# Holding the early loads of a retrieval kernel behind landings of its gathers

## The reference

```python
retrieved = jnp.mean(item_embeddings[indices], axis=1)       # 512 x 512, from 50 rows each
fused_input = jnp.concatenate([user_rep, retrieved], axis=1) # 512 x 1024
fused_rep = fused_input @ W_fuse + b_fuse                    # W_fuse 1024 x 512
logits = fused_rep @ W_proj + b_proj                         # W_proj 512 x 12500
```

## Time and profile before

| | |
|---|---|
| runs | 305.96, 305.21, 304.99 us |
| median | 305.21 us |
| the profiled execution's own time | 304.82 us |
| its span (first to last instruction) | 303.0 us |
| TensorE matmul busy | 290.6 us (96%) |
| VectorE busy | 242.4 us (80%) |
| ScalarE busy | 159.8 us (53%) |
| GpSimd busy | 73.1 us (24%) |
| DMA bytes moved | 75.14 MB |
| granted TensorE clock | 1.00 |

### The profile page before, as it was taken

How to read it: one execution, slowest core, us unless ns; L and a number is a source line. 1 busy time by engine, 2 the same in 40 slices (tenths; PEclk the granted TensorE clock), 3 DMA queues, 4 the chain that set the end, 5 groups by cost and what they waited for, 6 DMA issues and landing times.

```text
span 303.0 us, 4031 instructions
## 1 busy us (share of the span) xinstructions
PE 290.6 (96%) x1351; PEld 236.1 (78%) x1351; DVE 242.4 (80%) x355; ACT 159.8 (53%) x217; POOL 73.1 (24%) x76
## 2 busy tenths in 40 slices
PE   3996999999999999999999999999999999999995
PEld 1446887888888888888778888888888888888884
DVE  5897999668667789769998979979799797995133
ACT  3005665544544558968465685556845568453310
POOL 4785786777777100000000000000000000000000
PEclk9999999999999999999999999999999999999999
DMA  7999999896997247558875939749397493443315
GB/s 259 359 390 297 406 382 379 301 369 240 313 384 267 78 136 212 184 163 323 280 280 180 352 130 296 284 153 351 136 291 284 153 364 129 144 154 115 130 70 203
DMA packets 32480, 75.14 MB, mean 248 GB/s; under 512 B 4445, under 2 KB 20587, under 8 KB 32460
## 3 DMA queue, kind: packets, MB, share of 16 engines
q1 hardware_dynamic: 25340, 58.31, 54.6%
q0 software_dynamic: 5536, 13.73, 13.2%
q10 hardware_dynamic: 1584, 2.84, 2.5%
HBM read 52.84 MB, written 25.60 MB: 259 GB/s over the span
## 4 chain that ended last, share of the span: by engine, by line
PE 48%; DVE 3%; issue 1%; ACT 0%; DVEq 0%; ACTq 0%
PE pair L1273 16%; PE pair L1275 16%; PE pair L1276 16%; DVE w_lo L977 1%; DVE part_out L1002 0%; DVE out_sb L1002 0%; DVE t_sums L960 0%; DVE w_raw L968 0%; ACT odd_sum L653 0%; DVE out_sb L1135 0%; DVE t_sums L966 0%; DVE t_sums L972 0%; DVEq L998 0%; DVEq L971 0%; ACTq L648 0%
## 5 line engine op out<-in xcount | busy, mean ns | idle before, releaser
L446 POOL DMA_INDIRECT ring<-item_embeddings,rows x56 | 59.0, 1053 | 19.6 <-issue 13.7
L1273 PE MATMUL pair<-w_hi,s_hi 128*128 128x500 f32 x144 | 56.1, 390 | 0.5 <-ACT odd_sum L653 0.3
L1275 PE MATMUL pair<-w_lo,s_hi 128*128 128x500 f32 x144 | 56.0, 389 | 0.0
L1276 PE MATMUL pair<-w_hi,s_lo 128*128 128x500 f32 x144 | 55.8, 388 | 0.0
L1199 PE MATMUL pair<-w_hi,f_hi 128*128 128x500 f32 x112 | 44.3, 395 | 0.0
L1199 PE MATMUL pair<-w_lo,f_hi 128*128 128x500 f32 x112 | 43.8, 391 | 0.0
L869 DVE SCALAR_TENSOR_TENSOR pair<-ring,mask,pair 128x512 f32<-128x512 f32 x48 | 36.2, 754 | 9.4 <-DMA ring<-item_embeddings,rows 5.2
L1199 PE MATMUL pair<-w_hi,f_lo 128*128 128x500 f32 x112 | 43.5, 389 | 0.0
L1275 PE MATMUL pair<-w_lo,f_hi 128*128 128x500 f32 x108 | 42.0, 389 | 0.0
L1276 PE MATMUL pair<-w_hi,f_lo 128*128 128x500 f32 x108 | 41.9, 388 | 0.0
L1273 PE MATMUL pair<-w_hi,f_hi 128*128 128x500 f32 x108 | 41.8, 387 | 0.0
(11 more groups left out here) (142 smaller groups left out, 425.1 us busy)
## 6 DMA issues: line engine op xcount, KB each, us to landing
w_raw<-w_proj SPq DMA_DIRECT2D x28, 500.0 KB, 7.7
logits<-part_out SPq DMA_DIRECT2D x24, 500.0 KB, 3.2
early<-w_proj SPq DMA_DIRECT2D x22, 500.0 KB, 5.7
logits<-out_sb SPq DMA_DIRECT2D x23, 250.0 KB, 2.5
logits<-out_sb SPq DMA_DIRECT2D x11, 500.0 KB, 3.2
first_bias<-b_proj SPq DMA_DIRECT2D x10, 250.0 KB, 7.1
s_sum<-b_proj SPq DMA_DIRECT2D x8, 250.0 KB, 6.6
logits<-out_sb ACTq DMA_DIRECT2D x7, 250.0 KB, 7.2
```

The costliest lines, as they stand in the source:

```text
L446: return nc.gpsimd.indirect_dma_start(out=to, out_offset=None, in_=table, in_offset=bass.IndirectOffsetOnAxis(ap=column, axis=0), **how)
L1273: nc.tensor.matmul(ps[:, q, 0:CHUNK], f, hi, start=start and k == 0, stop=False, skip_group_check=True)
L1275: nc.tensor.matmul(ps[:, q, 0:CHUNK], f, lo, start=False, stop=False, skip_group_check=True)
L1276: m = nc.tensor.matmul(ps[:, q, 0:CHUNK], f_rest, hi, start=False, stop=stop and k == 1, skip_group_check=True)
```

## The change

SyncE's loads of the first stage no longer follow each other freely. After the first two quarters of the user part, each further group waits on SyncE until a gather of tile 0 has landed. The last two quarters of `user_t` are issued by SyncE and not by ScalarE. Chunk 0 is issued in two halves at different places, and `wf_ret` stands ahead of chunk 1. On VectorE the wait for `bias_lo_ready` moves from ahead of `add_home(0)` to behind its register load.

```diff
+USER_BEHIND = (0, 2)
...
-            def load_chunk(c):
-                for h in range(2):
+            def load_chunk(c, halves=(0, 1)):
+                for h in halves:
...
+            def behind_slot(i):
+                sp.wait_ge(slot_landed[place(0, i)], 16 * slot_uses(0, i))
+
             for k in range(HK):
+                if k >= HK // 2:
+                    behind_slot(USER_BEHIND[k - HK // 2])
+                    sp.dma_start(user_t[:, k, :], user_dram[k]).then_inc(user_landed[k], 16)
                 sp.dma_start(wf_user[:, k, :], wf_dram[0, :, k, :]).then_inc(wf_user_landed[k], 16)
                 if k == 0:
                     sp.dma_start(idx[:, K:TILES * K], indices[:, K:TILES * K]).then_inc(idx_landed, 16)
+            behind_slot(3)
+            load_chunk(0, (0,))
+            behind_slot(4)
             sp.dma_start(last_rows[:], last_item.to_broadcast([P, H])).then_inc(last_landed, 16)
-            load_chunk(0)
             sp.wait_ge(total_zeroed, 1)
...
             sp.dma_start(bf_col[:], b_fuse).then_inc(bf_landed, 16)
+            behind_slot(5)
+            load_chunk(0, (1,))
+            behind_slot(6)
+            sp.dma_start(wf_ret[:], wf_dram[1]).then_inc(wf_ret_landed, 16)
+            behind_slot(8)
             load_chunk(1)
-            sp.dma_start(wf_ret[:], wf_dram[1]).then_inc(wf_ret_landed, 16)
             sp.wait_ge(user_fused, 1)
-            sp.wait_ge(slot_landed[place(0, GATE)], 16 * slot_uses(0, GATE))
+            behind_slot(GATE)
...
         def _(act):
-            for k in range(HK):
+            for k in range(HK // 2):
                 act.dma_start(user_t[:, k, :], user_dram[k]).then_inc(user_landed[k], 16)
...
                 if t == 0:
                     dve.wait_ge(last_added, 1)
+                    dve.wait_ge(bias_lo_ready, 1)
...
             bias_lo()
-            dve.wait_ge(bias_lo_ready, 1)
             dve.wait_ge(laps_ready, 2)
             add_home(0)
```

## The result

The changed kernel takes 312.87 us (median of four runs, 312.57 to 313.3), beside 305.45 us for the kernel before: a ratio of 1.0243 [1.0222, 1.0265], or 7.4 us more. The forecast was 308.2 us, with a range up to 310.0. The direction was right; the size was not. The profiled execution of the changed kernel took 313.3 us, with a span of 311.4 us against 303.0.

What follows compares the result with a forecast made beforehand. It took the projections' start (35.23 us) and weight chunks arriving over a full bus as the bounds. The profiled 304.8 us plus 3.0 for late chunk 6 gave 307.8, plus 0.4 for the median 308.2; range 304.4 to 310.0.

Steps and rivals of the forecast that it cites:

- The start sets the end: TensorE from 33 us on: longest wait 0.3 us, so lateness at the projections' start (35.23 us) stays to the end.
- VectorE: Tile 0's tail: register load starts at 26.2 us, home add ends 0.7 us earlier, but the gain is lost behind ScalarE.
- The bus up to 14 us: Loads up to 14.0 us: 2.85 MB moved against 4.23 before, so 1.38 MB behind.
- The step that failed: Bus from 14 us on: no further gap, as gates open about 1.25 us apart with enough bytes behind each.
- 3.4 us of lost bus time: The 1.38 MB lag at 14 us, priced at 0.40 MB/us; bounds 2.1 to 4.8 us.
- The user parts: TensorE's third and fourth user parts, starting about 14.5 and 18.05 us: covered by quarters landing at 13.4 and 17.8 us.
- Chunk 1: End of the first stage's loads: chunk 1 lands at 31.4 us, so ScalarE's mean starts at 33.1, 1.9 us later.
- The chunks: Weight chunks up to 53 us: chunk 6 lands 3.0 us later, at 54.1, and TensorE waits another 1.1 us.
- the two delays do not add; the larger counts: Sum of the time: of the mean's 1.9 us and chunk 6's 3.0 us only the 3.0 is added.
- Rival 1: Early gathers pay and the lag is never felt: mean starts at 30.5 us, time 304.5 us; chance 0.22.
- Rival 2: Only ScalarE's wait counts: mean 1.9 us late, chunk 6 no later than TensorE, time 307.1 us; chance 0.13.
- Rival 3: Worse: gathers still take 7.9 us, gates open 3.7 us later, lag passes 4.8 us, 310 and more; chance 0.10.

Runs made afterwards that it cites:

- e1: The kernel before with only VectorE's part of the change (wait for bias_lo_ready behind the register load), loads issued as before: ratio 0.9979 to the kernel before.
- e12: The changed kernel with the load of the last row issued right behind the second quarter of W_fuse, ahead of every wait: ratio 1.0161 to the kernel before.
- e3: The changed kernel with the share of the last row and the mean ahead of chunk 1's casts on ScalarE: 311.52 us, ratio 1.0192 to the kernel before.
- e7: The changed kernel with chunk 1's casts behind mean and fuse parts on ScalarE, its low parts behind the fuse's on VectorE: 311.09 us, ratio 1.014.
- e10: The changed kernel with all its waits, but chunk 1 loaded ahead of the second half of W_fuse (wf_ret): ratio 1.0191 to the kernel before.
- e5: The changed kernel without the wait on slot 8 ahead of chunk 1, all other waits kept: 312.44 us, ratio 1.0179 to the kernel before.
- e6: The changed kernel with 18 small matmuls, results dropped, on TensorE between the list slot and the fuse: ratio 1.021 to the kernel before.

## Why the prediction was right in direction and too small in size

**The start sets the end.** Right: 7.9 us at the first projection are 8.4 us at the end of the span. The reading behind it was a little too strict: 0.3 us is the longest wait of a matmul, while weight loads waited up to 0.7 us.

**VectorE.** Right, and a little more: the register load runs ahead of its engine (it starts at 25.4 us, where 26.2 was taken), and alone (e1) the home add gains 0.93 us, where 0.7 was taken. In the changed kernel nothing of it is left, as said, though for a nearer reason than the one given: the lap gather lands too late.

**The bus up to 14 us.** The prediction had "1.38 MB behind at 14.0 us"; it was 1.12, as the gathers had moved 1.43 MB by then and not 1.18. Slot 0 landed at 8.3 where 9.15 was taken, slot 2 at 14.2 where 13.1 was the best case. This step held.

**The step that failed** is the next one: "From 14 us on I see no further gap: each gate opens about 1.25 us after the one before". From 14 to 28 us the changed kernel moved 4.16 MB (7.27 less 3.11), the kernel before 5.03. Most of that difference, 0.64 MB, is at 14 to 20 us, where the share was 0.86, so there was a gap. Its first part (0.33 MB) was SyncE's empty queue at 14 to 15.6 us: the wait on slot 2 opened 1.2 us after the best case, and the first bytes behind it followed more than another 1.3 us later, a time for which the prediction had no term. At 20 to 28 us the share was full in both kernels and neither moved 0.40 MB/us (305 and 334 GB/s); the earlier trace rows leave 20 to 26 us out, and the remaining 0.23 MB fell in this stretch. The lag became 1.99 MB, at 0.40 MB/us 5.0 us instead of the "3.4 us of lost bus time". Of the fall after 16 us e12 shows one cause, the load of the last row, which now ran there; the rest was not taken apart. The user parts stayed nearly covered: the fourth started at 19.91 instead of 18.05, after a wait of 1.2 us, and slots 9 and 10 were not there for another 9 us.

**Chunk 1.** "3.4 us later is 31.4 us" failed a second time. It let the late bytes have the bus to themselves. After 28 us gathers, 1.12 MB of them by 36.3 us, and chunk 2 (issued from 28.99 us on) run beside them: 28.0 + 5.0 is 33.0, but the last half of chunk 1 came at 36.2, another 3.2 us. So the mean was not "1.9 us later" but 6.6 (1.9 + 1.6 + 3.2 = 6.7 by these terms). The mechanism, ScalarE's order, was right and is shown by e3, e7 and e10.

**The fuse.** A term was missing: after standing still for 5.4 us TensorE came back at a granted clock of 0.72, which cost 1.3 us. 6.6 + 1.3 is the 7.9 us of the first projection.

**The chunks.** The prediction made chunk 6 the term of the sum, "3.0 us later", and said "the two delays do not add; the larger counts". The rule held, with the terms exchanged: in the changed kernel TensorE has no wait of over 0.5 us for a low part, since it comes to chunk 6 7.95 us late. Its first half landed at about 56.0 (issued at 46.22, 9.8 us), 1.9 later than the forecast of 54.1. With the first delay taken away (e7, where the casts are moved too) the chunks cost 6.6 us, so their term was undersized as well.

**The rivals.** Rival 1 fails: the early gathers did speed up, and the ones that are waited for did not. Rival 2 had the right bound, the late mean, with a third of its size (1.9 us for 6.6). Rival 3 had the time (310 and more), the late fourth user part and a lag above 4.8 us, but not the cause: "Gathers still take 7.9 us" fails for the gates ahead of the user part, which opened 0.8 us before (slot 0) and 1.2 us after (slot 2) the times of the forecast. Gathers issued from 16 to 22 us did take 8.3 to 9.6 us, but of the new gates only that of slot 8 stands behind one of them, and without it chunk 1 came no earlier (e5).

**Open.** What else beside the last row lowers the rate from 16 to 28 us, and why both kernels move only 305 to 334 GB/s at a full share from 20 to 28 us.

## What to carry to other kernels

A wait on a queue holds everything behind it, so price it by the bytes that the bus can't move any more, and then ask beside what those bytes will run later: the lag here grew from 1.12 to 1.99 MB after the last idle stretch seemed over. A wait that opens on an empty queue also costs the time until the first bytes, here more than 1.3 us. To see who pays, follow the last load on the queue to the first engine that takes work in a fixed order, and look at what stands behind it; here it was a mean that did not need the load at all. Holding back transfers speeds up the ones that run alone, which helps only if those are the ones that are waited for.

## What the runs showed of the hardware

- TensorE's granted clock: 0.72 in the 5.0 us after an idle time of 5.4 us, 0.53 in the 6.4 us of e10's fuse (after 3.3 us of idle time), and 1.00 where dummy matmuls filled 4.18 us of the gap (e6). From the fuse's first matmul to the first projection that took 4.9 and 6.4 us, at full clock 3.57.
- Gathers alone hold the bus engines without filling the bus: a share of 0.72 at 175 GB/s in 7 to 10 us.
- A busy bus is not always a full one: a share of 1.02 went with 305 GB/s at 20 to 28 us and a share of 1.03 with 401 at 28 to 36. The load of the last row went at 0.38 MB/us of bus time where no other load of SyncE's queue followed it (e12). Where others did, that queue reached 0.20 (changed kernel, beside gathers) and 0.19 (kernel before, with no gather).
- From the issue of a load on SyncE's queue, empty before, to the first bytes that this queue moves more than 1.3 us passed (14.26 to after 15.6 us, changed kernel).
- VectorE's register load starts at 25.4 us (e1), before the bias subtraction that stands ahead of it in the program and that starts at 26.1.
